# Attention and a two-layer local transformer on one normalized input: order planned by parts of one engine, PSUM banks chosen freely, the inner norm in token layout

## The chip, the cores and the metric

The kernel runs on one core of a Trainium2 chip. The metric is the device time of one execution in microseconds (us), from the first to the last instruction of the core and the little that lies around them. The engines are TensorE (PE; its weight loads are PEld in the profile), VectorE (DVE), ScalarE (ACT), GpSimd (POOL) and SyncE (SP), whose queue issues all DMAs of this kernel.

## The reference

The input is 16 images of 512 tokens with 128 features. Each is normalized over the features, and two branches of the normalized input are added to it.

```
xn = _layernorm(x)
# attention: 16 heads of 64, causal, biases
qkv = xn @ W_qkv + b_qkv;  probs = softmax(Q K / 8 + causal mask)
a = (probs @ V) @ W_out + b_out
# two layers, 8 heads of 64, windows of 64 tokens that look one window back
for l in range(2):
    h = shift_token(x)                      # half the features one token later
    q, k, v = split(h @ wqkv);  q = l2norm(q) * qs;  k = l2norm(k) * ksc
    q, k = rotary_xpos(q, k)
    x = x + local_attention(q, k, v) @ wo
    h = shift_token(x)
    h = (h - h.mean(-1)) / jnp.sqrt(h.var(-1) + 1e-05) * lg + lb
    a, g = split(h @ w1 + b1);  x = x + (a * gelu(g)) @ w2 + b2
out = x + a + y          # y: what the two layers make of xn
```

## The kernel before

All weights stay in SBUF. For one image the kernel has four streams of tasks: layer 0, layer 1, the front of the attention (`xt`, `a_proj`, `a_v`, `a_max`, `a_neg`) and its rest (`a_st`, `a_pv`, `a_ot`, `a_out`). A task is a group of TensorE instructions into one or more of the eight PSUM banks, and what other engines do with the result. `a_...` tasks run over eight pairs of heads, `f_...` tasks over a layer's four tiles of tokens or four pairs of heads. In the attention, `a_max` forms scores in bf16 for their row maxima, `a_neg` transposes the negated maxima, `a_st` forms the transposed scores in fp32 with masks and maxima added by further products, `a_pv` multiplies probabilities with values and a column of ones, `a_ot` transposes the result, `a_out` multiplies with `Wout`; VectorE sums the eight products in `aT_sum`, and the last into `aT`. A layer does the same with `f_q`, `f_k`, `f_v` (projection; for q and k ScalarE squares, VectorE multiplies with the rope tables and sums the squares, GpSimd raises the sums to the power -1/2 and multiplies), `f_qt` and `f_kt` (transposes), `f_max`, `f_neg`, `f_st`, `f_pv`, `f_ot`, `f_wo`.

The layer's inner norm works in feature layout, where a token is a column: `f_mean` (L1239) multiplies with a matrix that takes the mean off, ScalarE copies and squares the result, `f_var` (L1243) averages the squares by products, VectorE and GpSimd make 1/sqrt of it, `f_rep` (L1249) spreads that over the partitions, VectorE and ScalarE scale. Then `f_gate`, `f_up` and `f_down` form the gated feed-forward. `out` (L1273, L1274) transposes the attention's sum and the layers' result into one bank, eight transposes that add up; VectorE adds the input rows and SyncE stores.

TensorE uses the array in several tilings (`TILING`): whole, as two halves of rows (`a_max`, `a_st`, `f_max`), two halves of columns (`a_pv`, `f_pv`) and quarters (`f_st`).

The order is computed when the program is built. `least_idle` searches, over whole tasks, for one sequence `ORDER` of all streams with little modelled idle time on TensorE, from the durations in `STEPS`. Every engine goes through that one sequence, so that within an engine the work of a task follows that of the task before it. Banks are handed out in a ring: `Ring` gives claim number k the bank k modulo 8, whichever bank was read last. SyncE's queue is written out by hand: loads for the first image, a wait for GpSimd's constants, copies, all other weights and parameters, and only then the second image's `x_res`:

```
            sp.wait_ge(consts, CONSTS)
...
            weights(1)
            sp.sem_inc(stored, 16)
            psum.wait_filled(sp, 0, ("xt",), "x")
            load(x_res[:, :, :], slice(1, 2), x_loaded)
```

Of the kernel before, what the change touches and what calls it, by code (L numbers as in the profile page):

```python
# [17 lines left out]
P = 128  # L18
TILES = SEQ // P
HEAD = 64  # L20
# [24 lines left out]

A_ROUND = [("a_proj", 1), ("a_st", 0), ("a_ot", -1), ("a_max", 1), ("a_out", -1), ("a_pv", 0, 0),  # L50
           ("a_neg", 1), ("a_pv", 0, 1)]
# [5 lines left out]

RING = 8


def both(us):

    return [("pe", u, (), (2 * k, 2 * k + 1), ()) for k, u in enumerate(us)]


STEPS = {
    "norm": [("sp", 4.0, (), (), ()), ("dve", 2.0, (0,), (), ()), ("pool", 1.0, (1,), (), ()), ("dve", 1.4, (2,), (), ())],
    "xt": [("pe", 0.52, (), (0,), ()), ("act", 0.65, (0,), (), ()), ("dve", 0.75, (1,), (), (0,))],
    "a_proj": [("pe", 0.8, (), (0,), ()), ("pe", 0.74, (), (1,), ()), ("act", 0.72, (0,), (), (0,)), ("act", 0.72, (1,), (), (1,))],
    "a_v": [("pe", 0.86, (), (0,), ()), ("act", 0.62, (0,), (), (0,))],  # L70
    "a_max": both([0.22, 0.18, 0.24]) + [("dve", us, (b // 2,), (), (b,)) for b, us in enumerate((0.74, 0.74, 0.52, 0.52, 0.62, 0.62))],
    "a_neg": [("pe", 0.23, (), (0,), ()), ("act", 0.62, (0,), (), (0,))],
    "a_st": both([1.28, 1.28, 0.64]) + [("act", us, (b // 2,), (), (b,)) for b, us in enumerate((0.72, 0.6, 0.6, 0.6, 0.4, 0.4))],
    "a_pv": [("pe", 1.22, (), (0,), ()), ("dve", 0.65, (0,), (), (0,))],
    "a_ot": [("pe", 0.46, (), (0,), ()), ("act", 0.74, (0,), (), (0,))],
    "a_out": [("pe", 0.89, (), (0,), ()), ("dve", 0.74, (0,), (), (0,))],
    "f_first": [("pe", 0.52, (), (0,), ()), ("act", 1.25, (0,), (), (0,))],
    "f_q": [("pe", 0.89, (), (0,), ()), ("act", 0.62, (0,), (), ()), ("dve", 1.55, (1,), (), (0,)), ("dve", 0.7, (), (), ()),
            ("dve", 0.7, (), (), ()), ("pool", 2.45, (3,), (), ()), ("pool", 1.05, (4,), (), ())],
    "f_k": [("pe", 0.89, (), (0,), ()), ("act", 0.62, (0,), (), ()), ("dve", 1.55, (1,), (), (0,)), ("dve", 0.7, (), (), ()),  # L80
            ("pool", 2.3, (3,), (), ()), ("pool", 1.25, (2,), (), ()), ("pool", 1.05, (5,), (), ())],
    "f_v": [("pe", 0.87, (), (0,), ()), ("act", 1.8, (0,), (), (0,))],
    "f_qt": [("pe", 0.45, (), (0,), ()), ("act", 0.62, (0,), (), (0,))],
    "f_kt": [("pe", 0.45, (), (0,), ()), ("act", 0.62, (0,), (), (0,))],
    "f_max": both([0.2, 0.18]) + [("dve", 0.67, (b // 2,), (), (b,)) for b in range(4)],
    "f_neg": [("pe", 0.25, (), (0,), ()), ("act", 0.62, (0,), (), (0,))],
    "f_st": both([1.35]) + [("act", 0.62, (0,), (), (b,)) for b in range(2)],
    "f_pv": [("pe", 0.64, (), (0,), ()), ("dve", 0.65, (0,), (), (0,))],
    "f_ot": [("pe", 0.46, (), (0,), ()), ("act", 0.62, (0,), (), (0,))],
    "f_wo": [("pe", 3.45, (), (0,), ()), ("dve", 1.45, (0,), (), (0,))],  # L90
    "f_mean": [("pe", 0.87, (), (0,), ()), ("act", 1.25, (0,), (), (0,))],
    "f_var": [("pe", 0.9, (), (0,), ()), ("dve", 0.15, (0,), (), (0,)), ("pool", 0.95, (1,), (), ())],
    "f_rep": [("pe", 1.0, (), (0,), ()), ("dve", 0.8, (0,), (), (0,)), ("act", 0.75, (1,), (), ())],
    "f_gate": [("pe", 0.9, (), (k,), ()) for k in range(3)] + [("act", us, (k,), (), (k,)) for k, us in enumerate((2.0, 0.7, 0.6))],
    "f_up": [("pe", 0.9, (), (0,), ()), ("dve", 0.78, (0,), (), (0,))],
    "f_down": [("pe", 2.6, (), (0,), ()), ("dve", 1.55, (0,), (), (0,))],
    "out": [("pe", 1.82, (), (0,), ()), ("dve", 0.75, (0,), (), (0,))]}

TILING = {"a_max": "rows", "a_st": "rows", "f_max": "rows", "f_st": "quarters", "a_pv": "columns", "f_pv": "columns"}
CHANGE = 0.09  # L100

HOP = {"pe": 0.15, "act": 0.1, "dve": 0.15, "pool": 0.2, "sp": 0.1}
# [20 lines left out]


def layer_tasks(l):
# [8 lines left out]
A_FRONT = ("xt", "a_proj", "a_v", "a_max", "a_neg")  # L134
STREAMS = [layer_tasks(0), layer_tasks(1), [task for task in ATTENTION if task[0] in A_FRONT],
           [task for task in ATTENTION if task[0] not in A_FRONT]]
LAST_UP = len(HID_CHUNKS) - 1


def pair_before(i, kind, p, *rest):  # L140
# [1169 lines left out]
```

## Time and profile before

| | |
|---|---|
| median of 3 runs | 2985.31 us (2985.18 to 2985.89) |
| the profiled execution | 2985.46 us, its span 2983.6 us |
| TensorE busy | 2830.9 us (95%) |
| VectorE, ScalarE, GpSimd busy | 1993.4, 1695.7, 1016.1 us |
| mean granted TensorE clock | 0.99 of full speed |

A busy TensorE in these pages is counted to the modelled end of each matmul. Where matmuls follow each other in full flow, the next one starts before the end that is shown for the one before, so the distance from start to start is what a task takes of the engine.

### The profile page before, as it was taken

Reading aid. Unit: us, or ns where it says so; the run is one execution under the profiler, and the core shown is the slowest. Engines: PE = TensorE matmul, PEld = TensorE weight load, DVE = VectorE, ACT = ScalarE, POOL = GpSimd, SP = SyncE. Lnnn points to the kernel's source line nnn. Section 1 sums busy time; section 2 is a strip of 40 time slices with the busy share of each in tenths; the row PEclk is TensorE's granted clock in tenths of the full one; section 3 lists DMA queues with packets and bytes.
Section 4 is the critical chain, followed back from the end, with each engine's and each line's share of the span. In section 5 each row is a group of like instructions: output and inputs, shape, how many; then the busy total and the mean of one; then the engine's idle time right before and its main releaser. Section 6 shows DMA issues by size and latency. Waiting matters only on the chain.

```text
span 2983.6 us, 88168 instructions
## 1 busy us (share of the span) xinstructions
PE 2830.9 (95%) x34816; PEld 1898.3 (64%) x34816; DVE 1993.4 (67%) x6942; ACT 1695.7 (57%) x3094; POOL 1016.1 (34%) x995
## 2 busy tenths in 40 slices
PE   6999999999999999999999999999999999999986
PEld 4666566666666666666666666656666666666643
DVE  5667676666767666676766756667676776757743
ACT  5566565565556566555665655656565665656632
POOL 5134251433415143232432514334151432324331
PEclk9999999999999999999999999999999999999997
DMA  3000000000000000000000000000000000000000
GB/s 103 2 5 2 12 2 2 12 2 12 2 2 13 2 12 2 12 2 2 12 2 12 2 2 13 2 12 2 2 13 2 12 2 12 2 2 9 2 8 5
DMA packets 41711, 25.06 MB, mean 8 GB/s; under 512 B 13042, under 2 KB 40540, under 8 KB 41308
## 3 DMA queue, kind: packets, MB, share of 16 engines
q1 hardware_dynamic: 41308, 19.43, 2.3%
q8 instruction: 285, 4.67, 0.6%
q14 instruction: 118, 0.97, 0.1%
HBM read 14.96 MB, written 4.19 MB: 6 GB/s over the span
## 4 chain that ended last, share of the span: by engine, by line
PE 84%; DVE 5%; ACT 5%; issue 4%; POOL 2%; DMA 0%; POOLq 0%; ACTq 0%; DVEq 0%
PE bank L1130 10%; PE bank L1177 10%; PE bank L1047 7%; PE bank L1218 7%; PE bank L1203 4%; PE bank L1234 4%; PE bank L1190 3%; PE bank L1160 3%; PE bank L1223 3%; PE bank L1040 3%; PE bank L1266 3%; PE bank L1041 3%; PE bank L1042 3%; PE bank L1256 3%; PE bank L1261 3%
## 5 line engine op out<-in xcount | busy, mean ns | idle before, releaser
L901 DVE CUSTOM_DVE_ANT_0 bank<-bank,future 128x128 f32<-128x128 f32 (+3 forms) x1024 | 467.6, 528 | 102.5 <-PE bank L1089 102.2
L705 POOL TENSOR_TENSOR rnorm<-ssc,minus_half 128x8 f32<-128x8 f32 x256 | 426.5, 1666 | 21.3
L771 ACT ACTIVATE probs<-bank 128x512 f32<-128x512 f32 (+1 forms) x768 | 347.1, 532 | 149.2 <-PE bank L1139 148.4
L703 POOL TENSOR_SCALAR ssc<-ss 128x8 f32<-128x8 f32 x256 | 99.3, 388 | 973.4 <-DVE ss L961 969.9
L916 DVE CUSTOM_DVE_ANT_0 bank<-bank,band 128x192 f32<-128x192 f32 x1024 | 331.5, 396 | 120.2 <-PE bank L1107 119.3
L1130 PE MATMUL bank<-Qa,Ka 64*128 64x512 f32 (+3 forms) x2048 | 393.1, 466 | 7.9 <-ACT lprobs L778 3.0
L1177 PEld LDWEIGHTS bank<-Va,probs 128*64 128x64 f32 x10240 | 313.4, 138 | 62.8 <-issue 51.9
L1177 PE MATMUL bank<-Va,probs 128*64 128x65 f32 x10240 | 335.4, 223 | 1.8 <-ACT lprobs L778 0.8
L954 DVE TENSOR_TENSOR scratch<-bank,rope_t 128x512 f32<-128x512 f32 x256 | 176.6, 690 | 233.7 <-ACT scratch L798 203.7
L798 ACT ACTIVATE scratch<-bank 128x512 f32<-128x512 f32 x256 | 153.2, 599 | 267.6 <-PE bank L1218 194.3
L1218 PE MATMUL bank<-Lqkv,resid 128*128 128x512 f32 x512 | 274.6, 620 | 3.1 <-ACT resid L791 2.6
L778 ACT ACTIVATE lprobs<-bank 128x512 f32<-128x512 f32 x256 | 138.9, 595 | 148.6 <-PE bank L1165 148.3
L693 POOL TENSOR_TENSOR rstd<-var_eps,minus_half 128x4 f32<-128x4 f32 x16 | 16.2, 1012 | 606.6 <-DVE var_eps L866 606.6
L724 ACT ACTIVATE Qf<-bank 128x512 f32<-128x512 f32 x256 | 152.6, 604 | 73.1 <-PE bank L1047 72.0
L1130 PEld LDWEIGHTS bank<-Qa,Ka 64*128 64x128 f32 x2048 | 159.0, 188 | 37.4 <-issue 24.7
L1190 PEld LDWEIGHTS bank<-V_turned,lprobs 128*64 128x64 f32 x2048 | 136.4, 137 | 59.7 <-issue 37.6
L961 DVE TENSOR_REDUCE ss<-scratch 128x8 f32<-128x512 f32 x256 | 173.1, 676 | 0.0
L1190 PE MATMUL bank<-V_turned,lprobs 128*64 128x65 f32 x2048 | 166.3, 227 | 4.9 <-ACT lprobs L778 4.2
L1190 PE MATMUL bank<-Vf,lprobs 128*64 128x65 f32 x2048 | 166.4, 227 | 0.0
L709 POOL TENSOR_TENSOR scratch<-scratch 128x512 f32<-128x512 f32 x128 | 162.5, 1270 | 0.0
L916 DVE DVE_READ_ACCUMULATOR2_ANT negf<- 128x1 bf16 x1024 | 147.3, 144 | 0.1
L901 DVE DVE_READ_ACCUMULATOR2_ANT neg<- 128x1 bf16 x1024 | 146.8, 143 | 0.2
(163 smaller groups left out, 6564.8 us busy)
## 6 DMA issues: line engine op xcount, KB each, us to landing
x_res<-in_L_attn_x SPq DMA_DIRECT2D x16, 256.0 KB, 3.5
x_rows<-in_L_attn_x SPq DMA_DIRECT2D x16, 256.0 KB, 3.2
out<-yT SPq DMA_DIRECT2D x16, 256.0 KB, 2.4
Lqkv<-in_L_ffn_wqkv SPq DMA_DIRECT2D x2, 768.0 KB, 4.6
rope_t<-in_rope SPq DMA_DIRECT2D x8, 128.0 KB, 4.7
Kf<-in_L_attn_W_qkv SPq DMA_DIRECT2D x1, 768.0 KB, 7.4
Qf<-in_L_attn_W_qkv SPq DMA_DIRECT2D x1, 768.0 KB, 9.0
Lw<-in_L_ffn_w SPq DMA_DIRECT2D x2, 341.0 KB
```

Of the source, the lines that this page charges most:

```text
L705: g.tensor_tensor(rnorm[s][:, :], ssc[:, :], minus_half[:, :], ALU.pow).then_inc(rnorm_ready.sem, 1)
L709: g.tensor_tensor(turned, turn_a, turn_b, ALU.add).then_inc(turned_ready[c].sem, 1)
L771: psum.raise_read(a.activation(probs[j][:, at:at + n], psum.bank(i, task, (u, j))[:, 0:n], ACT.Exp, scale=float(HEAD) ** -0.5), i, task, ( ...
L901: ins = v.tensor_tensor_reduce(psum.bank(i, task, (u, j))[:, at:at + n], psum.bank(i, task, (u, j))[:, at:at + n], future[:, SEQ - n:SEQ], ...
L916: ins = v.tensor_tensor_reduce(psum.bank(i, task, (u, j))[:, k * BAND:(k + 1) * BAND], psum.bank(i, task, (u, j))[:, k * BAND:(k + 1) * BAND],
L954: v.tensor_tensor(heads(turn_a), src, table(0, 0, HEAD), ALU.mult)
L961: v.tensor_reduce(ss[s][:, :], heads(squares), AX.X, ALU.add).then_inc(sums_ready.sem, 1)
L1047: ins = nc.tensor.transpose(bank[:, t * P:(t + 1) * P], src(t), ident[:, :])
L1130: mm(bank[j][:, at:end], Ka[p % 2][HALF[j], tile(k)], Qa[p % 2][HALF[j], queries], start=True, stop=False)
L1177: ins = mm(bank[part, t * (HEAD + 1):(t + 1) * (HEAD + 1)], probs[j][:, at + part.start:at + part.stop], Va[p // 2 % 2][:, k, 2 * (p % 2) ...
L1190: ins = mm(bank[HALF[b % 2], t * (HEAD + 1):(t + 1) * (HEAD + 1)], lprobs[j][:, b * BLOCK:(b + 1) * BLOCK], V[:, t, 2 * p + j, :], start=T ...
L1218: psum.raise_filled(mm(bank[:, :], resid[l][:, tile(t)], Lqkv[l][:, c * INNER:(c + 1) * INNER], start=True, stop=True), i, task, kind[2])
```

## The change

`STEPS` becomes `PART_US`: each task is cut into parts, each on one engine, with the time for which it holds the engine and the later time at which its result is there. `parts_of_image` lists for each part what it comes after. `due_times` gives every part a due time (from the streams' offsets for TensorE, backwards from their users for the others, plus the corrections in `NUDGE`), and `in_order` lets each engine take in turn the open part that costs the least idle time and is due first. Each engine so has an order of its own (`ON[engine]`), and a claim takes the banks that were freed first (`SLOTS`). `a_max` and `a_st` can be taken apart between their steps. The order is still fixed when the program is built, and SyncE's queue is still written by hand.

The inner norm moves to token layout: `f_rows` transposes the residual, VectorE takes bn_stats and bn_aggr of the bank, GpSimd raises to -1/2, VectorE scales, `f_back` transposes back, ScalarE applies `lng` and `lnb`. `f_mean`, `f_var` and `f_rep` go. GpSimd adds `aT` to `yT` ahead of `out`, which has four transposes left. `a_out` adds two pairs of heads in one bank, so VectorE has four sums per image and not eight. The sum of the two rotary products moves to GpSimd for q as it was for k, and the buffers `squares`, `turn_a`, `turn_b`, `ssc`, `OaT` are doubled.

```
-ORDER = least_idle(40, (0.0, 1.4, 1.1, 1.2), 0.2, 0.05)
+OFFSETS = (0.0, 1.1, 0.878, 1.12)
+LAG, WASTE, SWITCH = 0, 1069.2, 0
+ORDER, SLOTS, SPAN = in_order(PARTS, due_times(PARTS, OFFSETS, LAG, NUDGE), WASTE, SWITCH)
...
+                worth = begin if engine == "dma" else due[event] + waste * (begin - clock[engine]) + cost
+                if best[engine] is None or (worth, number[event]) < best[engine][:2]:
+                    best[engine] = (worth, number[event], event, begin)
+        engine = min((e for e in HOP if best[e]), key=lambda e: best[e][3])
...
+        if engine == "pe":
+            tiling = part.tiling
+            slots[event] = [slot for _, slot in free[:part.banks]]
+            del free[:part.banks]
...
+    yield part(("dma", "x"), "in", [image(i - 1, ("xt",), "pe"), image(i - 1, ("f_first",), "pe")], extra=3.5)
+    yield part(("norm",), "stats", [here(("dma", "x"), "in")])
...
+            for i in range(1, BATCH + 2):
+                if i < BATCH:
+                    psum.wait_filled(sp, (i - 1, ("xt",), "pe"))
+                    psum.wait_filled(sp, (i - 1, ("f_first",), "pe"))
+                    load(x_res[:, :, :], slice(i, i + 1), x_loaded)
...
-                        v.tensor_tensor(turned, turn_a, turn_b, ALU.add).then_inc(turned_ready[c].sem, 1)
+                    elif part == "add":
+                        g.tensor_tensor(turn_a[s][k], turn_a[s][k], turn_b[s], ALU.add).then_inc(turned_ready.sem, 1)
+                elif kind == "out":
+                    g.tensor_tensor(yT[:, :], yT[:, :], aT, ALU.add).then_inc(sum_ready.sem, 1)
...
+                    stats_of(here, tiles_of(psum.bank(rows)[:, :]), lstats[l], lmv[l], lvar[l], rows_ready)
+                        ins = v.tensor_scalar(lrows[:, t, :], bank[:, t, :], lmv[l][:, t, 0:1], lrstd[l][:, t:t + 1], ALU.subtract, ALU.mult)
...
-                    for t in range(TILES):
-                        mm(bank[:, tile(t)], aT[:, tile(t)], ident[:, :], start=True, stop=False)
-                        ins = mm(bank[:, tile(t)], yT[:, tile(t)], ident[:, :], start=False, stop=True)
+                elif kind == "f_rows":
+                    transposes(here, lambda t: resid[2 * l][:, tile(t)], [((i, ("f_wo", l), "pe"), 0)])
+                elif kind == "f_back":
+                    transposes(here, lambda t: lrows[:, t, :], [((i, ("f_rows", task[1]), "pe"), 0)])
+                elif kind == "out":
+                    transposes(here, lambda t: yT[:, tile(t)])
```

The three places below show how instructions stand now. First VectorE at the very start of the program, from the last step of image 0's norm on. Before:

```order
6 L869 TENSOR_SCALAR x_res<-x_res,mv,rstd 128x128 [waits rstd_ready]
7 L869 TENSOR_SCALAR x_res<-x_res,mv,rstd 128x128 x3
8 L885 TENSOR_TENSOR Wqkv_lo<-Kf,Wqkv_hi 128x512 [waits staged0,split_hi] x3
9 L885 TENSOR_TENSOR Wqkv_lo<-Qf,Wqkv_hi 128x512 [waits staged1,split_hi] x3
10 L890 TENSOR_TENSOR xT_lo<-bank,xT_hi 128x512 [waits xt_ready,consts,split_lo]
11 L850 TENSOR_TENSOR rope_t<-rope_t,Qf 128x256 [waits rope_in0]
12 L850 TENSOR_TENSOR rope_t<-rope_t,Qf 128x256 x3
13 L954 TENSOR_TENSOR scratch<-bank,rope_t 128x512 [waits squares_ready,tables]
```

and with the change:

```order
7 L995 TENSOR_SCALAR x_res<-x_res,mv,rstd 128x128 x3
8 L1000 TENSOR_TENSOR xT_lo<-bank,xT_hi 128x512 [waits xt_ready]
9 L962 BN_STATS stats<-x_res 128x6 [waits norm_ready,x_loaded]
10 L962 BN_STATS stats<-x_res 128x6 x3
11 L966 BN_AGGR mv<-stats 128x2 [waits norm_ready]
12 L966 BN_AGGR mv<-stats 128x2 x3
13 L969 TENSOR_SCALAR var_eps<-mv 128x4 [waits norm_ready]
14 L986 TENSOR_TENSOR rope_t<-rope_t,Qf 128x256 [waits rope_in0]
15 L986 TENSOR_TENSOR rope_t<-rope_t,Qf 128x256 x3
16 L1050 TENSOR_REDUCE ss<-squares 128x8 [waits squares_ready]
17 L1063 TENSOR_TENSOR turn_a<-bank,rope_t 128x512 [waits tables,squares_ready]
18 L1066 TENSOR_TENSOR turn_b<-bank,rope_t 128x8x32
```

Statistics of the next image's `x_res`, with their wait for `x_loaded`, now stand fourth among VectorE's steps; the `Wqkv_lo` rows, which were next after the norm, start six rows behind those shown.

The second place is SyncE's queue at the end of the start-up loads. Before:

```order
43 L577 DMA Lw<-in_L_ffn_w 128x128 x2
44 L577 DMA Lw<-in_L_ffn_w 85x128
45 L557 DMA x_res<-in_L_attn_x 128x4x128 [waits bank1_filled]
46 L557 DMA x_rows<-in_L_attn_x 128x4x128
47 L557 DMA x_res<-in_L_attn_x 128x4x128 [waits bank5_filled]
48 L622 DMA out<-yT 128x4x128 [waits bank7_read]
```

and with the change:

```order
43 L688 DMA Lw<-in_L_ffn_w 128x128 x2
44 L688 DMA Lw<-in_L_ffn_w 85x128
45 L668 DMA x_res<-in_L_attn_x 128x4x128 [waits bank0_filled,bank1_filled]
46 L668 DMA x_res<-in_L_attn_x 128x4x128 [waits bank4_filled,bank1_filled]
47 L668 DMA x_rows<-in_L_attn_x 128x4x128
48 L733 DMA out<-yT 128x4x128 [waits bank4_read]
```

The 44 rows ahead of the first `x_res` shown are the same loads in both; what moved is `x_res` of the images behind it against `x_rows` and the stores.

The third place is the end of TensorE's queue. Before, from the last layer's `f_wo` on:

```order
9186 L1234 MATMUL bank<-Qf,Lwo 128x512 x4
9187 L1239 MATMUL bank<-resid,center 128x512
9188 L1243 MATMUL bank<-mean_of,ff 128x2 x4
9189 L1249 MATMUL bank<-ident,lrstd 128x128 x4
9190 L1256 MATMUL bank<-lT,Lw 128x512 x2
9191 L1256 MATMUL bank<-lT,Lw 85x512
9192 L1261 MATMUL bank<-lT,Lw 128x512 x2
9193 L1261 MATMUL bank<-lT,Lw 85x512
9194 L1266 MATMUL bank<-GLU,Lw 128x512 x3
9195 L1273 MATMUL bank<-ident,aT 128x128
9196 L1274 MATMUL bank<-ident,yT 128x128
```

and with the change:

```order
8742 L1235 MATMUL bank<-later_k,row_of 128x128 x2
8743 L1145 MATMUL bank<-ident,ff 128x128 x4
8744 L1271 MATMUL bank<-Va,probs 64x65 x40
8745 L1332 MATMUL bank<-lT,Lw 128x512 x2
8746 L1332 MATMUL bank<-lT,Lw 85x512
8747 L1337 MATMUL bank<-lT,Lw 128x512 x2
8748 L1337 MATMUL bank<-lT,Lw 85x512
8749 L1145 MATMUL bank<-ident,Oa 128x128 x4
8750 L1298 MATMUL bank<-OaT,Wout 128x512 x2
8751 L1343 MATMUL bank<-ff,Lw 128x512 x3
8752 L1145 MATMUL bank<-ident,yT 128x128 x4
```

Before, the attention's last product with `Wout` (L1203) stands 132 rows ahead of the rows shown; now the last pairs' `a_st`, `a_pv` (L1271), transposes of `Oa` and the last `a_out` (L1298) stand between `f_rows` and `f_down` of the last layer.

## Rows read from the trace of the kernel before

**Rows 1.** The page: span, busy time by engine, issues to landing.

```profile
span 2983.6 us, 88168 instructions
PE 2830.9 (95%) x34816; PEld 1898.3 (64%) x34816; DVE 1993.4 (67%) x6942; ACT 1695.7 (57%) x3094; POOL 1016.1 (34%) x995
x_res<-in_L_attn_x SPq DMA_DIRECT2D x16, 256.0 KB, 3.5
```

**Rows 2.** Windows: busy us by engine in each stretch, then granted clock, DMA.

```profile
0.00:25.00 25.00, 3.99 (x10) 2.07 (x10) 7.66 (x21) 6.89 (x11) 17.85 (x52) 1.00 0.48 132
60.00:2860.00 2800.00, 2712.10 (x33800) 1825.79 (x33796) 1914.71 (x6705) 1629.80 (x2981) 955.89 (x903) 1.00 0.02 6
2880.00:2984.00 104.00, 62.66 (x500) 35.24 (x498) 40.28 (x127) 30.36 (x51) 30.71 (x29) 0.77 0.03 8
```

**Rows 3.** Groups by line: busy us, mean ns | idle before, releaser.

```profile
L966 DVE TENSOR_TENSOR scratch<-scratch 128x512 f32<-128x512 f32 x128 | 87.2, 681 | 0.0
L709 POOL TENSOR_TENSOR scratch<-scratch 128x512 f32<-128x512 f32 x128 | 162.5, 1270 | 0.0
L859 DVE BATCH_NORM_STATS2 stats<-x_res 128x6 f32<-128x128 f32 x64 | 13.9, 281 | 3.9 <-DMA x_res<-in_L_attn_x 3.5
L869 DVE TENSOR_SCALAR x_res<-x_res,mv,rstd 128x128 f32<-128x128 f32 x64 | 17.8, 342 | 18.1 <-POOL rstd L693 18.1
L696 POOL TENSOR_TENSOR lrstd<-lvar,minus_half 128x4 f32<-128x4 f32 x32 | 32.3, 1010 | 289.3 <-DVE lvar L976 289.3
```

**Rows 4.** Timeline of TensorE, 131 to 143 us: start, us, instruction.

```profile
134.98 1.13 PE L1239 MATMUL bank<-resid,center 128*128 128x512 f32 x2
135.94 0.60 PE L1047 MATMUL bank<-ident,Oa 128*128 128x128 f32 x4
137.28 1.05 PE L1243 MATMUL bank<-mean_of,ff 128*128 128x2 f32 x8 [0.74 <-ACT ff L826]
138.20 1.10 PE L1203 MATMUL bank<-OaT,Wout 128*128 128x512 f32 x2
...
140.55 1.16 PE L1249 MATMUL bank<-ident,lrstd 128*128 128x128 f32 x8
141.64 1.39 PE L1177 MATMUL bank<-Va,probs 128*64 128x65 f32 x40
```

**Rows 5.** Timeline of TensorE around an output task.

```profile
352.79 0.49 PE L1273 MATMUL bank<-ident,aT 128*128 128x128 f32 x2
...
354.68 1.02 PE L1218 MATMUL bank<-Lqkv,resid 128*128 128x512 f32 x2
```

**Rows 6.** Timeline of TensorE, tasks in full flow.

```profile
1285.43 1.02 PE L1223 MATMUL bank<-Lqkv,resid 128*128 128x512 f32 x2
1286.29 1.02 PE L1203 MATMUL bank<-OaT,Wout 128*128 128x512 f32 x2
1287.24 0.97 PE L1177 MATMUL bank<-Va,probs 128*64 128x65 f32 x25
```

**Rows 7.** Timeline of SyncE's queue at the start.

```profile
50.14 0.39 SPq L557 DMA_DIRECT2D x_res<-in_L_attn_x  x1
```

**Rows 8.** Timeline of VectorE at the start.

```profile
18.48 2.35 DVE L885 TENSOR_TENSOR Wqkv_lo<-Qf,Wqkv_hi 128x512 fp32r<-128x512 f32 x3
...
24.82 1.42 DVE L850 TENSOR_TENSOR rope_t<-rope_t,Qf 128x256 f32<-128x256 f32 x4
```

**Rows 9.** Timeline of TensorE at the start.

```profile
25.05 0.77 PE L1040 MATMUL bank<-xT_hi,Wqkv_hi 128*128 128x512 f32 x1 [11.70 <-DVE xT_lo L890]
```

**Rows 10.** Last product with Wout, and the last microseconds of all engines.

```profile
L1203 PE MATMUL bank<-OaT,Wout x256: 590/592/697, 54.2 to 2879.2; 128*128 128x512 f32 x128
...
2980.21 0.69 DVE L1029 TENSOR_TENSOR yT<-bank,x_rows 128x512 f32<-128x512 f32 x1 [2.23 <-PE bank L1274]
2980.93 0.38 SPq L622 DMA_DIRECT2D out<-yT  x1
```

**Rows 11.** TensorE's waits from 2880 us on.

```profile
PE bank L1047 <- POOL kn L714: 10.7, 4, 3.4
```

More of the change, by code:

```diff
@@ new lines @@
+ENGINE_OF = dict(early="pool", rest="pool", hi="act", lo="dve", turn="dve", stats="dve", pow="pool", scale="dve", q="pe", k="pe", q_out="act", k_out="act",
+                 max="dve", exp="act", pe="pe", square="act", mult="pool", add="pool", sum="dve")
+ENGINE_AT = {("a_pv", "out"): "dve", ("f_pv", "out"): "dve", ("out", "out"): "dve", ("out", "sum"): "pool", ("f_wo", "add"): "dve", ("f_up", "mult"): "dve",
+             ("f_down", "add"): "dve"}
+TILING = {"a_max": "rows", "a_st": "rows", "f_max": "rows", "f_st": "quarters", "a_pv": "columns", "f_pv": "columns"}
@@ L56 @@
            ("f_v", 3), ("f_qt", 3), ("f_kt", 3)]
[L58 to L97, printed above, removed]
@@ L122, in attention_round @@
     return out
 def layer_tasks(l):
-    start = [("norm",), ("f_first",)] if l == 0 else []
-    tail = [(kind, l) for kind in ("f_wo", "f_mean", "f_var", "f_rep", "f_gate")] + [("f_up", l, j) for j in range(len(HID_CHUNKS))]
-    return start + [(kind, l, t) for kind, t in F_FRONT] + rounds(F_ROUND, LPAIRS, (l,)) + tail + [("f_down", l)] + \
-        ([("out",)] if l == DEPTH - 1 else [])
-ATTENTION = [("xt",)] + [task for r in range(-1, PAIRS + 1) for task in attention_round(r)]
-A_FRONT = ("xt", "a_proj", "a_v", "a_max", "a_neg")
@@ L288 @@
[L288 to L309 removed]
+    tail = [(kind, l) for kind in ("f_wo", "f_rows", "f_back", "f_gate")] + [("f_up", l, j) for j in range(len(HID_CHUNKS))] + [("f_down", l)]
@@ new lines, in image, with __init__ @@
+def image(i, task, part):
+    return (i, task, part) if i >= 0 else None
+class Part:
+    def __init__(self, event, after, banks, gives, begun, extra):
+        _, task, part = event
+        kind, step = task[0], part.rstrip("0123456789")
+        self.event, self.banks = event, banks
+        self.engine = "dma" if kind == "dma" else ENGINE_AT.get((kind, step), ENGINE_OF.get(step, "act"))
+        self.us, self.late = (0.0, extra) if kind == "dma" else PART_US[kind][part]
+        self.after = [e for e in after if e is not None]
+        self.begun = [e for e in begun if e is not None]
+        self.gives = gives
+        self.tiling = TILING.get(kind)
+        self.table = TABLE.get((kind, step))
@@ L1143, in _ @@
+                        last = [mm(bank[j][:, at:at + P], row_of[HALF[j], 1, :], later_k[HALF[j], :],
+                                   start=False, stop=True) for j in range(2)]
+                    for j in range(2):
+                        psum.raise_filled(last[j], here, j)
                 elif kind == "f_st":
                     _, l, p = task
-                    if i == 0 and task == ("f_st", 0, 0):
+                    if is_first(here, "a_st", "f_st"):
                         pe.wait_ge(halved, HALVED)
-                    after = [(("f_neg", l, p), "m")]
```

1346 lines of the change are left out of this document (714 added, 632 removed).

## The prediction, made before the changed kernel ran

> **What bounds the kernel.** I read the page first, then the windows, then TensorE's timeline and its waits. TensorE is busy for 2830.9 of 2983.6 us, the next engine for 1993.4 [rows 1], so the time is TensorE's work plus what it waits. The windows say where it waits: in the first 60 us, where weights still arrive; a little everywhere in the middle (2800 us with 2712.1 busy); and in the last 104 us, which hold 62.7 busy at a mean granted clock of 0.77 [rows 2]. The busy figures are not the price of the work, because each matmul is counted to a modelled end. A `L1223` task is shown with 1.02 us, and the next task starts 0.86 after it [rows 6]. So I price work by the distance from start to start, in places where nothing is waited for. A change of tiling also has a price: the `L1203` task does the same 1024 columns as the `L1223` task, and the quarter- or half-tiled task behind it starts after 0.95 instead of 0.86 [rows 6]. That is 0.09 per change, and the order before has 1,313 changes. Priced so, task by task with the pitch of its kind, the 2800 us of the middle hold 2501 us of work, 119 of changes and **182 of waits**, twice the 88 that show as idle. The first 60 us hold 31 of work and 29 that is not. The last 104 hold 42 of work.
>
> **The change part by part.** The profiled run is 2985.46 us, 1.9 more than its span; the median is 0.15 less. I sum against the run.
>
> *The layer's tail.* `f_mean` holds TensorE for 135.94 − 134.98 = 0.96 us, `f_var` for 0.92, `f_rep` for 1.09 [rows 4]. Two changes of tiling that stand in these three gaps are counted below, so 2.97 − 0.18 = 2.79 goes. `f_rows` and `f_back` are four transposes each; the `L1223` task has 1024 columns in 0.86 [rows 6], four transposes of 128 columns are half of that, 0.43, and both tasks 0.87. That is −1.92 in each of 32 layer tails: −61. `out` took 354.68 − 352.79 = 1.89 [rows 5], 1.80 without its change of tiling, and now takes 0.44: −1.36 × 16 = −22. Together **−83**.
>
> *Tilings.* The new order has 919 changes, 394 fewer, at 0.09 [rows 6]: **−35**.
>
> *VectorE, GpSimd, ScalarE.* VectorE loses the q sum (87.2 us, 128 instructions) [rows 3], four `aT` sums per image (about 0.69 each, 44) and the scaling of the feature layout (about 29), and gains bn_stats (128 × 0.28 and up to 0.4 if a bank reads slower), bn_aggr and the scaling of 128 tiles (0.34 to 0.41 each) [rows 3]: 1993 becomes about 1940. GpSimd gains 128 + 16 sums at 1.27 [rows 3]: 1016 becomes 1199. ScalarE falls by some 38. All three stay far below TensorE, so these cost nothing where other work covers them. The cover of the new norm is the products between `f_rows` and `f_back`: at least 4.05 us and mostly 7.0 of TensorE work by the new order, against stats 4 × 0.28 + aggregates, one power at 1.01 and scaling 4 × 0.34 [rows 3], about 4.9 with the hops. If a tail had no cover it would cost 4.9 × 32 = 157.
>
> A row shows GpSimd's sum of two SBUF tiles at 1.27 and VectorE's at 0.68 [rows 3]: 272 GpSimd sums instead of 128, all of SBUF, are +183 us of GpSimd and −87 of VectorE. The Trainium skill speaks against such a move. "SBUF — State Buffer" (Who interferes with whom) says that a VectorE instruction with two SBUF inputs and a GpSimd instruction that reads SBUF exclude each other, and "Perfetto Trace Analysis" (Optimizing Scalar/DVE Operations) that offloading between the two may not help. By it, the sum of this kernel would lose what each blocked VectorE step makes late; no row of before isolates a blocked step. The mechanism has a rival of its own below.
>
> *The start.* Here the change adds a wait. SyncE issues the second image's `x_res` at 50.14 [rows 7], behind 44 rows of loads, and a transfer lands 3.5 later [rows 1]. Before, VectorE needed it long after. Now the statistics of that load stand fourth in VectorE's queue. With three constants fewer I take the issue at 49 and the landing at 52.5. Behind the wait stand the rest of that norm, the rope tables (1.42), then `Wqkv_lo` (2.35 and 1.99) [rows 8], and without `Wqkv_lo` the first `a_proj` can't run. Stats 1.5, tables 1.4, two sums 1.3, two turned products 2.5 and 4.3 for `Wqkv_lo`: `a_proj` starts near 63.6 and not at 25.05 [rows 9], 38.6 later. TensorE can in the meantime do seven projections of layer 0 (7 × 0.86 = 6), then the eight banks are full and it idles: **+33**. If the load came as early as the order supposes, this would be 0.
>
> *The end.* Before, the last `a_out` starts at 2879.2 [rows 10], and 104 us follow for 42 of work, because a single stream is left whose steps wait for each other: `kn` of GpSimd alone is waited for four times, 10.7 us [rows 11]. In the new order the last heads' `a_st`, `a_pv` and `a_out` stand between `f_rows` and `f_down` of the last layer. What is then left alone is a chain of the sum with b2s, GpSimd's sum 1.27, transposes, a sum of 0.69 and the store, whose issue is 2980.93 of 2983.6 [rows 10]: some 12 us. So of the 62 us that were not work about 12 stay: **−50**.
>
> *The middle.* What the freed order gives is the least sure term. No row of before shows it; I read the orders for the TensorE work between the product that starts a chain and the task that needs its end. From `f_neg` to `f_st` the median rises from 1.5 us to 9.6, `f_max` to `f_neg` from 3.2 to 8.6, `a_neg` to `a_st` from 3.5 to 5.1, projections to their users from 6 to 12.6; `f_mean` to `f_var` with 0.4 in a quarter of cases is gone (a wait of 0.74 for `ff` shows in [rows 4]). Two distances shrink: `a_st` to `a_pv` 7.5 to 6.4, `a_pv` to `a_ot` 8.7 to 3.9. A wait for a bank that the ring named while another was free can't occur any more. The bounds are all waits kept (0) and nearly all gone (−150). I take half of the 182: **−92**, in the visible idle of that window [rows 2] some 44 of 88.
>
> Sum: 2985.5 − 83 − 35 + 33 − 50 − 92 = **2758.5**.
>
> **Rivals.** *The freed order saves no waits in the middle.* For it: the order is as much a plan with guessed durations as the old one, and it repeats for each image, so one wrong guess costs fifteen times. Against it: the distances. The time is 2758.5 + 92 = 2850.
>
> *The start costs nothing.* For it: weights are loading anyway, and the layer's tasks might carry TensorE on. Against it: eight banks fill. The time is 2758.5 − 33 = 2725.
>
> *GpSimd's sums block VectorE.* If each of 272 sums held VectorE for its whole 1.27 [rows 3], 345 us would be added to VectorE, 2290 in all; still under TensorE, so only steps with short cover turn into waits. I price it at one TensorE wait of 0.3, half the difference of 1.27 and 0.68, for each of the 128 sums that moved: 40, which gives 2798. This is also the time that the rule of the Trainium skill named above would give here.
>
> *Slower than before.* Each engine now has an order of its own that interleaves all streams, and none can take a ready step past a late one. If the steps' real durations differ from the table, TensorE waits at each crossing. This decides from 2985.5 − 83 − 35 + 33 − 50 = 2850 with all of the old waits kept: another 135 us on top of 182, in the middle alone. Over some 3,600 TensorE tasks that is 0.04 us a task more than the 0.05 of now, or 0.09 in all. For it: GpSimd's queue now holds sums of two streams. Against it: a third of each engine but TensorE is idle.
>
> **How the numbers follow.** Chances: the forecast 0.60, no waits saved 0.15, the start free 0.12, GpSimd blocking 0.08, slower 0.05. The forecast's own range is 2705 to 2815, from the middle at −150 to −35. To hold the time 8 times in 10 I take 2700 to 2850: it takes in the free start and the blocking, up to the edge of the case without savings. A change within 0.2% (6 us), about what a measurement of this kernel can't tell from none, would need an unlikely balance: 0.01. Faster 0.94, slower 0.05.
>
> **What would show it.** VectorE idles in the profile of the changed kernel for `x_res` from about 8 to 52 us, and the first `a_proj` starts past 60. PE's busy time falls by some 85 to 120 us. The last `a_out` starts within 20 us of the end, and the last slice of granted clock is above 0.9. GpSimd's busy time is near 1200, VectorE's near 1940. Waits of TensorE between 100 and 2700 us stay below 60 visible us. I'm wrong if `f_back` waits for `lrows` in most layers (the norm has no cover), if `a_ot` waits for `Oa` (distance 3.9), or if VectorE's sums lengthen beside GpSimd's.

## The result, and the profile after

The changed kernel takes 2738.1 us (median of 4 runs, 2737.7 to 2738.3) against 2985.6 for the kernel before: a ratio of 0.917, with a 95% interval of 0.9153 to 0.9185, 247 us less. The forecast was 2758, with a range of 2700 to 2850.

The page of the changed kernel, to be held against [rows 1]:

```profile
span 2736.5 us, 89709 instructions
PE 2656.3 (97%) x34304; PEld 1821.8 (67%) x34304; DVE 1928.7 (70%) x7102; ACT 1656.7 (61%) x3030; POOL 1147.0 (42%) x1136
PEclk6999999999999999999999999999999999999999
```

TensorE's busy time fell by 174.6 us and its share rose to 97%. VectorE fell to 1929 (1940 was said) and GpSimd rose to 1147 (1199 was said). In the third row the last of the forty slices has a granted clock of 0.9, where the last 104 us of [rows 2] had 0.77.

The windows of the changed kernel, with the columns of [rows 2]:

```profile
0.00:25.00 25.00, 10.47 (x24) 5.12 (x24) 3.23 (x14) 5.93 (x9) 16.35 (x49) 0.99 0.49 133
25.00:60.00 35.00, 0.00 (x0) 0.00 (x0) 6.61 (x22) 2.26 (x5) 1.76 (x3) 0.50 0.45 115
60.00:2640.00 2580.00, 2557.59 (x32944) 1754.39 (x32946) 1865.40 (x6853) 1604.47 (x2935) 1126.62 (x1083) 1.00 0.02 7
2640.00:2737.00 97.00, 88.27 (x1344) 62.34 (x1340) 53.46 (x215) 44.06 (x82) 2.28 (x2) 0.97 0.02 5
```

In the middle TensorE is visibly idle for 2580 − 2557.6 = 22.4 us, where it was 88. The last 97 us hold 88.3 of busy time; the last 104 before held 62.7. And from 25 to 60 us TensorE does nothing at all, where the kernel before was already at work:

```profile
25.00:60.00 35.00, 33.43 (x348) 23.95 (x350) 23.65 (x77) 21.23 (x39) 11.64 (x12) 1.00 0.48 126
```

TensorE and VectorE at the start of the changed kernel, in the form of [rows 8, 9]:

```profile
11.31 8.53 PE L1307 MATMUL bank<-Lqkv,resid 128*128 128x512 f32 x16 [1.87 <-ACT resid L911]
63.52 0.80 PE L1138 MATMUL bank<-xT_hi,Wqkv_hi 128*128 128x512 f32 x1 [43.68 <-DVE Wqkv_lo L980]
```

```profile
11.82 0.69 DVE L1000 TENSOR_TENSOR xT_lo<-bank,xT_hi 128x512 fp32r<-128x512 f32 x1 [4.46 <-ACT xT_hi L849]
53.32 0.87 DVE L962 BATCH_NORM_STATS2 stats<-x_res 128x6 f32<-128x128 f32 x4 [40.81 <-DMA x_res<-in_L_attn_x]
```

VectorE stands for 40.8 us in front of the second image's `x_res`; behind it stand the tables and `Wqkv_lo`, and TensorE, after eight projections of layer 0 in eight banks, waits 43.7 us for `Wqkv_lo`.

The end, on TensorE:

```profile
2723.83 1.98 PE L1298 MATMUL bank<-OaT,Wout 128*128 128x512 f32 x4 [0.84 <-ACT OaT L902]
2725.65 2.74 PE L1343 MATMUL bank<-ff,Lw 128*128 128x512 f32 x6
2731.82 1.12 PE L1145 MATMUL bank<-ident,yT 128*128 128x128 f32 x4 [3.43 <-POOL yT L829]
```

The last `a_out` (L1298) starts 12.7 us before the end of the span; in [rows 10] the last one started 104.4 before it.

The waits of TensorE between 100 and 2640 us (line, waited for, us in all, times, longest); the list's three longest entries:

```profile
PE bank L1282 <- DVE Oa L1042: 4.0, 12, 0.4
PE bank L1226 <- DVE Oa L1042: 3.3, 12, 0.3
PE bank L1253 <- issue: 1.7, 4, 0.7
```

Next in the list `f_back` waits once, 0.8 us, for its rows (the new norm is covered). No matmul waits for a result of GpSimd there.

### The profile page after: what moved, and what is told of

Its sections match the earlier page's. It is cut to its first block, busy times and chain, and to the rows that moved or that the text cites. A ratio compares the mean times of both kernels' runs of the same rounds, so it can differ in the third digit from the quotient of the medians.

```text
span 2736.5 us, 89709 instructions
## 1 busy us (share of the span) xinstructions
PE 2656.3 (97%) x34304; PEld 1821.8 (67%) x34304; DVE 1928.7 (70%) x7102; ACT 1656.7 (61%) x3030; POOL 1147.0 (42%) x1136
## 4 chain that ended last, share of the span: by engine, by line
PE 87%; DVE 7%; issue 3%; POOL 1%; SPq 1%; ACT 0%; DMA 0%; DVEq 0%; POOLq 0%; ACTq 0%
PE bank L1307 12%; PE bank L1226 12%; PE bank L1145 10%; PE bank L1271 9%; PE bank L1298 4%; PE bank L1321 4%; PE bank L1282 4%; PE bank L1253 4%; PE bank L1332 3%; PE bank L1343 3%; PE bank L1138 3%; PE bank L1337 3%; PE bank L1140 3%; PE bank L1139 3%; PE bank L1186 3%
## 5 line engine op out<-in xcount | busy, mean ns | idle before, releaser
L816 POOL TENSOR_TENSOR rnorm<-ssc,minus_half 128x8 f32<-128x8 f32 x256 | 431.4, 1685 | 21.3
L819 POOL TENSOR_TENSOR turn_a<-turn_a,turn_b 128x512 f32<-128x512 f32 x256 | 325.3, 1274 | 138.5 <-DVE turn_b L1067 138.2
L1307 PE MATMUL bank<-Lqkv,resid 128*128 128x512 f32 x768 | 367.9, 599 | 2.7 <-ACT resid L911 1.9
L1271 PEld LDWEIGHTS bank<-Va,probs 128*64 128x64 f32 x10240 | 310.0, 138 | 26.4 <-issue 24.5
L1271 PE MATMUL bank<-Va,probs 128*64 128x65 f32 x10240 | 325.4, 223 | 1.0 <-DVE negf L1027 0.3
L823 POOL TENSOR_TENSOR turn_a<-turn_a,rnorm 128x512 f32<-128x512 f32 x256 | 263.7, 1043 | 1.4
L1063 DVE TENSOR_TENSOR turn_a<-bank,rope_t 128x512 f32<-128x512 f32 x256 | 175.6, 686 | 77.6 <-ACT squares L917 76.8
L917 ACT ACTIVATE squares<-bank 128x512 f32<-128x512 f32 x256 | 153.6, 601 | 101.3 <-PE bank L1307 57.0
L1307 PEld LDWEIGHTS bank<-Lqkv,resid 128*128 128x128 f32 x768 | 134.8, 191 | 111.5 <-issue 101.4
L1226 PEld LDWEIGHTS bank<-Qa,Ka 64*128 64x128 f32 x2048 | 160.6, 187 | 28.3 <-issue 23.9
L1050 DVE TENSOR_REDUCE ss<-squares 128x8 f32<-128x512 f32 x256 | 171.6, 676 | 3.3 <-POOL rnorm L816 3.2
L1138 PE MATMUL bank<-xT_hi,Wqkv_hi 128*128 128x512 f32 x256 | 121.9, 476 | 43.9 <-DVE Wqkv_lo L980 43.7
L1145 PEld LDWEIGHTS bank<-ident,turn_a 128*128 128x128 f32 x1024 | 116.4, 140 | 55.3 <-issue 43.0
L1145 PE MATMUL bank<-ident,turn_a 128*128 128x128 f32 x1024 | 152.0, 277 | 0.6 <-DVE negf L1027 0.3
```

Source lines behind the costliest of these rows:

```text
L816: g.tensor_tensor(rnorm[s][:, :], ssc[s][:, :], minus_half[:, :], ALU.pow).then_inc(rnorm_ready.sem, 1)
L819: g.tensor_tensor(turn_a[s][k], turn_a[s][k], turn_b[s], ALU.add).then_inc(turned_ready.sem, 1)
L823: g.tensor_tensor(heads(turn_a[s][k]), heads(turn_a[s][k]), rnorm[s][:, :].unsqueeze(2).broadcast_to([P, LHEADS, HEAD]), ALU.mult).then_in ...
L1138: mm(dst, left[0], right[0], start=True, stop=False)
L1145: ins = nc.tensor.transpose(bank[:, t * P:(t + 1) * P], src(t), ident[:, :])
L1226: mm(bank[j][:, at:end], Ka[p % 2][HALF[j], tile(k)], Qa[p % 2][HALF[j], queries], start=True, stop=False)
```

## The experiments

All times are medians; differences are to the changed kernel's 2738.1 us. The experiments ran in three groups, later than the changed kernel. The kernel before, which ran beside each group, had medians from 2985.6 to 2990.8 us there, and its single runs spread by up to 8.7 us within a group. Differences of 5 us and less are therefore not resolved.

### The start: one wait, then the wait behind it

**load_early.** SyncE issues the second image's `x_res` ahead of its wait for the constants.

```
+            psum.wait_filled(sp, (0, ("xt",), "pe"))
+            psum.wait_filled(sp, (0, ("f_first",), "pe"))
+            load(x_res[:, :, :], slice(1, 2), x_loaded)
             sp.wait_ge(consts, CONSTS)
...
-                if i < BATCH:
+                if 1 < i < BATCH:
```

> The changed kernel with one edit: SyncE issues the second image's x_res before its wait for GpSimd's constants. No engine's order changes. If the statistics of that load stop VectorE at the start and everything behind them (the forecast's reading; 40.8 us of VectorE idle for x_res in the profile after, first a_proj at 63.5), the load lands near 20 us, a_proj starts near 28 to 30 and the time falls by 33 to 36 us to about 2703. If the start is bound by the arrival of the weights or by anything else that this wait only covered, a_proj starts past 45 and less than 15 us come back (above 2723).

Measured: 2725.6 us, 12.5 less. The first `a_proj` came at 30.9, close to the 28 to 30 expected, but the gain of 33 to 36 did not come. TensorE of this kernel:

```profile
30.89 0.79 PE L1141 MATMUL bank<-xT_hi,Wqkv_hi 128*128 128x512 f32 x1 [9.51 <-DVE Wqkv_lo L983]
...
53.22 0.55 PE L1141 MATMUL bank<-Wqkv_hi,xT_hi 128*128 128x256 f32 x1 [18.38 <-DVE turn_b L1070]
```

and VectorE and SyncE's queue:

```profile
28.95 1.88 DVE L983 TENSOR_TENSOR Wqkv_lo<-Kf,Wqkv_hi 128x512 fp32r<-128x512 f32 x3
50.38 0.76 DVE L989 TENSOR_TENSOR rope_t<-rope_t,Qf 128x256 f32<-128x256 f32 x2 [19.55 <-DMA Qf<-in_L_ffn_k_scale]
...
44.08 1.38 SPq L681 DMA_DIRECT2D Qf<-in_L_ffn_k_scale  x3
```

A second wait stood hidden behind the first: layer 1's rope tables are next in VectorE's queue after `Wqkv_lo`. Their loads are issued from 39 to 45 us, while the planner's table has them arrive at 22.

**plan_late.** SyncE's queue stays; the planner is told that this `x_res` comes late, and so orders its statistics 38th in VectorE's queue.

```
-    yield part(("dma", "x"), "in", [image(i - 1, ("xt",), "pe"), image(i - 1, ("f_first",), "pe")], extra=3.5)
+    yield part(("dma", "x"), "in", [image(i - 1, ("xt",), "pe"), image(i - 1, ("f_first",), "pe")], extra=43.0 if i == 1 else 3.5)
```

> The changed kernel with one number in the planner's input: the second image's x_res is taken to arrive 43 us after it may be issued and not 3.5. SyncE's queue stays, but VectorE's order has these statistics 38th and not fourth. The forecast's reading: the same gain as with the early load, 30 to 36 us, time 2702 to 2708. Rival: TensorE's orders differ too, and the second image's front comes later, so that only half comes back (about 2720).

Measured: 2726.1 us, 12.0 less, for the same reason: the first `a_proj` is at 23.4, and then TensorE waits 25.9 us for `turn_b` behind the tables. Both expectations missed in the same way.

**both_early.** As load_early, and `turn_tables(1)` is moved to the same place.

```
             load(x_res[:, :, :], slice(1, 2), x_loaded)
+            turn_tables(1)
             sp.wait_ge(consts, CONSTS)
```

> The changed kernel with x_res of the second image and the ten loads of layer 1's rope tables issued ahead of SyncE's wait for the constants; no engine's order changes. With x_res alone early, VectorE went on to a second wait in its queue, 19.6 us for layer 1's k_scale rows (issued at 44 us), and TensorE idled 18.4 us for turn_b behind it. If the start's cost is these two queued waits, this kernel loses both: first a_proj near 31, no TensorE wait over 5 us before 60 us but for the first ones, time 2725.6 - 15 to 20, that is 2706 to 2711. If a third load stands behind (layer 0's parameters, the masks), it stays above 2718.

Measured: 2704.8 us, 33.4 less (ratio to the kernel before 0.904, interval 0.9031 to 0.9058), 1.2 below the expected range. The second load is worth 20.8 once the first is out of the way. The longest wait of TensorE between the first `a_proj` at 31.0 and 60 us is 1.1 us.

**planned_early.** SyncE's queue as in both_early, and the planner is told the arrivals that go with it.

```
-    yield part(("dma", "x"), "in", [image(i - 1, ("xt",), "pe"), image(i - 1, ("f_first",), "pe")], extra=3.5)
+    yield part(("dma", "x"), "in", [image(i - 1, ("xt",), "pe"), image(i - 1, ("f_first",), "pe")], extra=11.0 if i == 1 else 3.5)
...
-ARRIVES = dict(wqkv=11.3, rope0=13.0, rope1=22.0, staged0=15.6, staged1=17.6)
+ARRIVES = dict(wqkv=11.3, rope0=13.0, rope1=26.0, staged0=15.6, staged1=17.6)
```

> The candidate for the fastest version: both_early's queue for SyncE, and the planner told when these loads arrive (the second image's x_res 11 us after it may be issued, layer 1's tables at 26 us), so that neither stands in VectorE's queue ahead of Wqkv_lo. First a_proj then at 23 to 25 as with plan_late, 6 us earlier than in both_early: 2697 to 2701. Rival: what is gained at the first a_proj is lost at the next wait for weights or banks, since all loads still end near 50 us: 2702 to 2708, no better than both_early's 2704.8.

Measured: 2701.8 us (2700.0 to 2701.8), 36.3 less, ratio to the kernel before 0.904 with an interval of 0.9025 to 0.9055. The first `a_proj` is at 23.9. That lies between the expectation and its rival. It has the lowest time of the study, but its lead over both_early, 3.0 us, is not resolved: both have the ratio 0.904 to the kernel before.

### The middle: whose order is it?

**lockstep.** TensorE's order and banks stay word for word. The other engines go through their parts in the order of the TensorE parts that these follow, as all engines did before the change.

```
+def lockstep(order):
+    at, seen = {}, 0
+    for event in order:
+        part = PARTS[event]
+        free = part.engine == "dma" or event[1][0] in ("consts", "split", "tables", "norm", "out")
+        if part.engine == "pe":
+            seen += 1
+            at[event] = seen
+        else:
+            at[event] = max([seen * free] + [at[e] for e in part.after + part.begun])
+    return sorted(order, key=lambda event: (at[event], PLACE[event]))
+ORDER = lockstep(ORDER)
```

> The changed kernel's TensorE order and banks, word for word, but VectorE, ScalarE and GpSimd go through their parts in the order of the TensorE parts that they follow (norm, out's sum, tables and the split of Wqkv keep their places). Theory A: the orders of their own of the other engines save most of the waits in the middle, so these come back: 2738 + 60 to 120, that is 2800 to 2860. Theory B: TensorE's own order and its longer distances between producers and users save them, the other engines' orders matter little: 2738 + 0 to 20.

Measured: 2916.4 us, 178 more, beyond even theory A's range. TensorE's longest waits in it between 100 and 2800 us; all are for steps of VectorE (`Of` is the scaled result of `f_pv`, `neg` the row maxima of `a_max`, `turn_b` a rotary product):

```profile
PE bank L1266 <- DVE Of L1060: 25.2, 13, 2.0
PE bank L1163 <- DVE Of L1060: 21.9, 32, 2.9
PE bank L1289 <- DVE neg L1030: 19.3, 13, 1.5
PE bank L1233 <- DVE Of L1060: 13.2, 13, 1.0
PE bank L1204 <- DVE turn_b L1085: 12.8, 13, 1.0
```

**lockstep_dve.** Only VectorE's order is taken from lockstep; ScalarE and GpSimd keep theirs.

```
+TOGETHER = lockstep(ORDER)
+ON = {engine: [event for event in (TOGETHER if engine in ("dve",) else ORDER) if PARTS[event].engine == engine] for engine in HOP}
```

> As lockstep (which cost 178 us), but VectorE alone goes in the order of the TensorE parts; ScalarE and GpSimd keep their own orders. TensorE's waits in lockstep ended nearly all with VectorE's steps (Of, turn_b, neg). If VectorE's queue is the one that needed its own order, nearly all of the loss is here too: 2870 to 2920. If it takes all three engines out of order to lose it, under 2830.

Measured: 2882.2 us, 144 more: with VectorE's queue alone in lockstep, four fifths of the loss are there. The 178 us are what this order of TensorE loses without queues to match. They are not a share of the 247: no run has the old order of TensorE with free queues.

**lockstep_ring.** As lockstep, with the banks of the old ring.

```
+claimed = 0
+for event in ORDER:
+    if event in SLOTS:
+        SLOTS[event] = [(claimed + j) % RING for j in range(len(SLOTS[event]))]
+        claimed += len(SLOTS[event])
```

> As lockstep, with claim number k of a bank given bank k modulo 8 as before the change, whichever bank was read last. If a bank named by the ring is often still in use while another is free, this costs a further 10 to 40 us over lockstep, and TensorE's waits name readers of old banks. If eight banks turn so fast that the order of reading is the order of claims, it costs under 5 us.

Measured: 2959.0 us, 42.6 more than lockstep, a little above the expected 10 to 40. The ring with the changed kernel's own orders has no run. Followed through the planned orders, its waits close in a circle, since a bank is then named whose reader stands behind a part that needs this very claim. The same holds for ScalarE and GpSimd in lockstep with VectorE free. Free banks are thus worth 43 us in lockstep, and these separate orders can't be had without them.

**no_nudge.** The planner runs with `NUDGE = {}`.

> The changed kernel planned with no corrections of due times (NUDGE empty); 987 changes of tiling, 68 more. Theory A, that each engine's own order is what matters and the corrections polish it: 2738 + 6 to 13 for the changes of tiling and as much again for waits, under 2775. Theory B, that the gain hangs on corrections fitted to this order: above 2800.

Measured: 2743.4 us, 5.2 more, at the edge of what is resolved and less than theory A's 12 to 26. The corrections are a polish; the gain doesn't hang on them.

### TensorE's work and its tilings

**pe_padded.** Own orders, with transposes repeated into the same bank.

```
-                for t in range(TILES):
+                for _ in range({"out": 4, "f_rows": 3, "f_back": 3}.get(here[1][0], 1)):
+                    for t in range(TILES):
```

> The changed kernel in its own order, but f_rows and f_back transpose three times into their bank and out four times, so that TensorE has again about the work that the old norm and out had: 32 x 4 x 0.43 + 16 x 3 x 0.43 = 76 us more, the result unchanged. If TensorE's work is what the time is made of, as the forecast's -61 and -22 assume, the time is 2738 + 76 = 2814, within 6. If part of it lies in idle time that TensorE has anyway, it is below 2795; if the longer tasks make other waits, above 2830.

Measured: 2809.5 us, 71.4 more for 76 of work: 94% of the added work shows in the time. By the ratios to the kernel before (0.9395 against 0.9169) it is 67 us, 89%.

**tiling_alone** and **tiling_tasks.** TensorE alone; nothing of the reference is computed. Groups of two tilings in turn, and then the same groups sorted.

```
                if alternate:
                    for n in range(N):
                        one(2)
                        other(4)
                else:
                    for n in range(N):
                        one(2)
                    for n in range(N):
                        other(4)
```

> TensorE alone, fp32 products that are always ready, of which nothing but a copy is stored (it computes nothing of the reference): 100 groups of four full-array products in turn with 100 groups of products in halves of rows, halves of columns or quarters, then the same groups sorted, so that only the number of changes of tiling differs (199 against 1 in each pair of stretches). The forecast's price is 0.09 us a change: the mixed stretch lasts 18 us longer than the sorted one. If the price seen in the kernel was that of something else at these places (weights, banks), the two last the same within 2 us.

> As tiling_alone (it computes nothing of the reference), with products of the kernel's own sizes: one product of 512 columns, four of 128, four of 512 columns in halves of rows, twenty of 65 columns in halves of columns, in turn or sorted, 198 changes more in the mixed stretch. With the short groups before, a change cost 0.17 to 0.19 us, half of it at the change (0.205 instead of 0.112 from start to start) and half behind the product after it. If the second half is hidden behind long products, pairs with the product of 512 columns show 0.09 to 0.10 a change; if a change always costs both, 0.17 to 0.19 in every pair, and the forecast's term for 394 changes was half of what it should be.

Two pieces of TensorE's timeline of tiling_tasks, from the mixed and from the sorted stretch of one pair (a product of 512 columns at L60, four of them in halves of rows at L74):

```profile
199.79 1.12 PE L60 MATMUL bank<-keys,rows 128*128 128x512 f32 x2
200.85 1.99 PE L74 MATMUL bank<-keys,rows 64*128 64x512 f32 x8
202.76 1.13 PE L60 MATMUL bank<-keys,rows 128*128 128x512 f32 x2
...
372.24 86.10 PE L60 MATMUL bank<-keys,rows 128*128 128x512 f32 x200
458.27 171.94 PE L74 MATMUL bank<-keys,rows 64*128 64x512 f32 x800
630.14 1.12 PE L60 MATMUL bank<-keys,rows 128*128 128x512 f32 x2
```

Mixed, a pair of groups takes 202.76 − 199.79 = 2.97 us. Sorted, it takes (630.14 − 372.24) / 100 = 2.58. Two changes of tiling cost 0.39, one 0.19. Over whole stretches the nine pairs of the two kernels gave 0.167 to 0.198 a change, with short products and with long ones. The spacing of the records shows the two halves: the next group starts 0.09 late behind the last pass of a group, and the first pass of the new group is followed 0.10 late (0.533 instead of 0.43 for 512 columns). The second half stays with the task *behind* the change. So 0.09 at the change was right, but tiling_alone's expectation of 18 us between a mixed and a sorted stretch was not: they differ by 33 to 39. Of tiling_tasks' two answers the second held, that a change always costs both halves. Both halves are shown as busy time: from 60 to 1200 us of tiling_alone TensorE is busy for 1139.3 of 1140.

The kernel before shows the same. Here an `L1218` task stands behind one in halves of rows and ahead of transposes, which use the whole array:

```profile
1105.40 0.74 PE L1089 MATMUL bank<-Ka,Qa 64*128 64x128 bf16 x8
1106.07 1.13 PE L1218 MATMUL bank<-Lqkv,resid 128*128 128x512 f32 x2
1107.03 0.60 PE L1047 MATMUL bank<-ident,qn 128*128 128x128 f32 x4
```

From its start to the next is 0.96, where the `L1223` task of [rows 6], with the same columns and no change on either side, takes 0.86. It is also shown as 1.13 long and not 1.02. This half was thus in the trace of before. The Trainium skill says in "TensorEngine Tiling (Array Packing)" (Key Properties) that a change of the tiling mode drains TensorE. It gives no number; the traces agree that a change costs time, with the 0.167 to 0.198 us above.

### GpSimd beside VectorE

**q_dve.** q's sum goes back to VectorE.

```
-             ("f_down", "add"): "dve"}
+             ("f_down", "add"): "dve", ("f_q", "add"): "dve"}
...
+                    elif part == "add":
+                        k = (TURN[i, l] * TILES + t) % 2
+                        psum.wait_read(dve, (i, task, "pe"))
+                        v.tensor_tensor(turn_a[s][k], turn_a[s][k], turn_b[s], ALU.add).then_inc(turned_ready[kind].sem, 1)
```

> The changed kernel with q's sum of the two turned products on VectorE again (0.68) and k's on GpSimd, planned anew with the same corrections; TensorE has 934 changes of tiling for 919. VectorE then has again 128 steps with two SBUF inputs beside GpSimd. If GpSimd and VectorE hold each other up, these steps spread far above 0.68 and GpSimd's sums above 1.27 where they meet, and the time gains or loses by it. If not (VectorE's steps kept their durations in the profile after, 0.69 for L1063 as 0.69 for L954 before), the steps last 0.68, VectorE's busy time rises by 87 us, and the time moves only by what the new plan costs: within 25 us of 2738, above it.

Measured: 2777.7 us, 39.6 more, outside the expected 25. The steps that came back lasted 0.83 on average, in groups by line (columns as in [rows 3]):

```profile
L1055 DVE TENSOR_TENSOR turn_a<-turn_a,turn_b 128x512 f32<-128x512 f32 x128 | 105.8, 827 | 0.5
L819 POOL TENSOR_TENSOR turn_a<-turn_a,turn_b 128x512 f32<-128x512 f32 x128 | 169.7, 1326 | 50.0 <-DVE turn_b L1072 49.9
```

Their median is 0.683 and their longest 1.557. One of the long ones, with what GpSimd did then:

```profile
821.29 1.43 DVE L1055 TENSOR_TENSOR turn_a<-turn_a,turn_b 128x512 f32<-128x512 f32 x1
822.65 0.17 DVE L1039 RECIPROCAL rec_a<-bank 128x4 f32<-128x4 f32 x1
...
821.12 1.05 POOL L823 TENSOR_TENSOR turn_a<-turn_a,rnorm 128x512 f32<-128x512 f32 x1
```

VectorE's sum starts inside GpSimd's product, and ends 0.55 us behind it: GpSimd's remaining 0.88 us and then most of its own 0.68. Of these steps 16 met L823 products alone. Each began inside one and ended 0.55 behind it, and their mean was 1.33. Where VectorE reads one operand from a bank (L1063 in the changed kernel), it kept 0.69 under the same steps of GpSimd (18 of them met L823 alone, mean 0.690). The Trainium skill says in "SBUF — State Buffer" (Who interferes with whom) that a VectorE instruction with two SBUF inputs contends with a GpSimd instruction that reads SBUF, and one with at most one such input does not. The trace agrees for L823 (1.33 and 0.690). It differs for GpSimd's power of eight columns (L816), which reads SBUF too: 17 of VectorE's sums met it alone, 16 of them begun while it ran, and lasted 0.69. Whether its reading was over by then, the trace does not show.

The kernel before had the block as well, on GpSimd's side. All 128 of VectorE's sums stayed at 0.68 there, and each had begun ahead of the clipping step L703 that it met. Of those clipping steps 127 lasted 0.53 to 0.54, while the 128 that met none lasted 0.24. In the changed kernel, without such sums, all last 0.24 (L814):

```profile
L703 POOL TENSOR_SCALAR ssc<-ss 128x8 f32<-128x8 f32 x256 | 99.3, 388 | 973.4 <-DVE ss L961 969.9
L814 POOL TENSOR_SCALAR ssc<-ss 128x8 f32<-128x8 f32 x256 | 61.6, 241 | 47.4 <-DVE ss L1050 47.4
```

Where two steps block each other in these traces, the one that begins second waits.

What of the 39.6 us is this and what is the new plan can't be told from this run: the lengthening adds 19 us to VectorE's busy time, 15 more changes of tiling are about 3 us of TensorE, and TensorE's matmuls wait 10.6 us for GpSimd's `turn_a`, which in the changed kernel none does. At the start the new plan puts more of VectorE's steps ahead of `Wqkv_lo`, and the first `a_proj` comes at 66.5 and not at 63.5.

## Why the prediction was right, step by step

The mechanism and the sign hold, and the time is within the forecast's own range. By its terms:

- **The layer's tail and `out`, −83.** Held. `f_rows` and `f_back` take 0.44 us from start to start (median), `out` 0.43, for the 0.43 and 0.44 forecast, and by pe_padded's 94% the term is worth about 78.
- **Tilings, −35.** The count (919 changes) was right, the price half of the true one. I read 0.09 from one row where a task *ends* before a change, and missed the 0.10 in the task behind it. With 0.167 to 0.198 the 394 changes are worth 66 to 78 us, an estimate: no run changes only the tilings of the kernel, and no_nudge, with 68 changes more, lost 5.2 us where this price asks for 11 to 13. By ratio this term was mis-sized most.
- **The start, +33.** The numbers held: first `a_proj` at 63.52 for 63.6, and both_early gives back 33.4 (with its first `a_proj` still 6 us later than before the change; planned_early, without that, gives back 36.3). But the sentence that an early `x_res` would make this 0 failed: it gives back 12.5. A second queued wait, for layer 1's tables, was behind it, and I had checked only the first wait in the queue.
- **The end, −50.** Held by the profile: visible idle time fell from 41.3 to 8.7 us in the last hundred, and the mean clock there is 0.97 and not 0.77. No run isolates this term.
- **The middle, −92.** The visible idle time fell by 65 us, from 88 to 22.4. The 182 us of waits that I had worked out held the missed half of 1,313 changes, 101 to 142 us, which leaves 40 to 81 for waits proper. As 88 were visible, the upper end is the nearer, and most of them are gone. The −92 was thus too large for waits, and the tilings more than make up for it: −92 and −35 make 127, the two pieces found 65 and about 72. That the two errors nearly cancel is luck; the forecast of the sum was better than that of these terms.

The pieces −78, −72, +33, −50 (as forecast) and −65 make −232; 15 of the 247 us have no place yet; waits that the busy time hides are a guess that no run tests. Two slips in the sums change nothing here: 2800 − 2501 − 119 is 180 and not 182, and with the middle at −150 the range begins at 2700 and not at 2705.

Of the rivals, *no waits saved* is refuted by the windows, *the start costs nothing* by both_early, and *slower* by the result. *GpSimd's sums block VectorE* is wrong for this change but for a reason that the forecast didn't see: past the start VectorE has no sum left with two operands in SBUF, because the change moved the last kind of them away. q_dve shows the block where such steps exist. The forecast used the rule against the move, and it speaks for it. Nor was it right that no row of before isolates a blocked step: L703 does, with its two durations.

"PE's busy time falls by 85 to 120" missed: it fell by 174.6. Counted with it are 83 of work, some 72 for the changes of tiling, both halves of which are shown as busy, and about 20 at the end, where 42 us of work filled 62.7 at the lower clock. GpSimd's 1147 instead of 1199 comes mostly from its clipping step, which VectorE's sums no longer hold up: 0.24 instead of 0.39 us in the mean, 256 times.

The middle's argument was weak in another way too. I argued with distances on TensorE; lockstep has the same distances, and is 178 us slower. What it loses lies mostly in where the steps stand in VectorE's queue (lockstep_dve).

## What to carry to other kernels

Price a mode change from a mixed and a sorted stretch, or from both sides of it in the trace: half of its cost can lie in the task behind. When a wait at the head of an in-order queue is taken away, look at once at the next entries for a load that the plan supposes too early; each must be compared with the time at which the issuing queue really reaches it. Let each engine have its own order with banks chosen by what is free, VectorE first of all; and, where GpSimd has time left, give it those elementwise steps whose operands both lie in SBUF, and VectorE those that read a bank.

## What the runs showed of the hardware

A change of tiling cost TensorE 0.17 to 0.20 us, with short products and with long ones, between the whole array and each of the three other forms and between halves of rows and of columns (quarters against halves was not tried). A VectorE step with both operands in SBUF that began during a GpSimd product lasted up to 1.56 us instead of 0.68, while one that reads a bank kept 0.69. The other way round, a clipping step of GpSimd that began during such a VectorE step lasted 0.54 instead of 0.24. After TensorE's 43.7 us of idle time the granted clock was 0.50 in the window to 60 us, which is its lower level; `a_proj`'s products of 512 columns then stood 0.43 us apart (64.11 to 64.54), and 0.23 from 68.8 us on.
